# Gated cross-attention with a ternary FFN: the first two turns as one list, ternary weights by a sign, and spare TensorE products

## The reference

```
x = x + tanh(g_xattn) * attn(layernorm(x), ctx, ctx, mask)      # 16 heads of 32, 77 keys per batch
x = x + tanh(g_ffn)   * ffn(layernorm(x))

attn: q, k, v = query Wq^T, ctx Wk^T, ctx Wv^T;  softmax(masked q k^T / sqrt(32)) v;  times Wo^T
ffn:  down(silu(gate(z)) * up(z)), each a "bitlinear", 512 -> 2048 -> 512
  act_quant(x):    s = 127 / max(|x| over features); round(x s) clipped, / s
  weight_quant(w): s = 1 / mean(|w|); clip(round(w s), -1, 1) / s
```

## Time and profile before

| | us |
|---|---|
| median of 3 runs | 1346.26 (1342.62 to 1346.9) |
| profiled execution | 1347.23, of which the span of instructions is 1345.4 |
| TensorE (PE) busy | 1253.8 (93%) |
| VectorE (DVE) busy | 1122.8 (83%) |
| ScalarE (ACT) busy | 870.6 (65%) |
| GpSimd (POOL) busy | 737.6 (55%) |
| mean granted TensorE clock | 0.974 of full speed |

### The profile page before, as it was taken

One profiled execution on the slowest core, in us unless ns is written; L12 is line 12 of the kernel. 1 busy time (PEld: TensorE's weight loads), 2 busy tenths in 40 slices (PEclk: granted clock), 3 DMA queues, 4 the chain that ended last, 5 costly groups with the idle time before them and its releaser, 6 DMA issues.

```text
span 1345.4 us, 26267 instructions
## 1 busy us (share of the span) xinstructions
PE 1253.8 (93%) x7552; PEld 620.8 (46%) x8126; DVE 1122.8 (83%) x2631; ACT 870.6 (65%) x1350; POOL 737.6 (55%) x1186
## 2 busy tenths in 40 slices
PE   4767699999999999999999999999999999999996
PEld 2223344445454454545454454545445454544542
DVE  6777597897979898897979899797979889796883
ACT  4886756658584766757575665757475665857562
POOL 2104654647475564657466564757566465747662
PEclk9867899999999999999999999999999999999998
DMA  9785348565665658564674756565574847565432
GB/s 327 234 253 114 72 80 172 115 151 115 130 138 111 146 117 169 114 147 113 122 158 89 172 117 150 116 143 124 109 155 109 179 106 152 113 133 98 87 83 67
DMA packets 386793, 181.64 MB, mean 135 GB/s; under 512 B 324323, under 2 KB 357987, under 8 KB 385123
## 3 DMA queue, kind: packets, MB, share of 16 engines
q1 hardware_dynamic: 386736, 181.04, 60.0%
HBM read 61.32 MB, written 35.46 MB: 72 GB/s over the span
## 4 chain that ended last, share of the span: by engine, by line
PE 52%; DVE 18%; DMA 12%; issue 6%; ACT 5%; SPq 4%; POOL 2%; POOLq 0%; ACTq 0%; DVEq 0%
PE bank L1247 16%; PE bank L1259 11%; PE bank L1107 6%; PE bank L1108 6%; PE bank L1109 6%; DMA aT<-ah 6%; PE bank L1186 4%; DVE nmax L987 4%; DVE region L1048 3%; DMA xT<-xh 2%; DVE ah L1011 2%; DVE hmx L1054 2%; POOL work L621 1%; DVE xn L972 1%; ACT work L744 1%
## 5 line engine op out<-in xcount | busy, mean ns | idle before, releaser
L630 POOL TENSOR_TENSOR region<-region,up 128x512 f32<-128x512 f32 x256 | 328.4, 1288 | 290.9 <-DVE region L1048 197.6
L1247 PE MATMUL bank<-tern_gate,region 128*128 128x512 fp8e4 x1024 | 264.6, 381 | 12.3 <-DMA region<-zb 9.3
L1247 PE MATMUL bank<-tern_up,region 128*128 128x512 fp8e4 x1024 | 263.7, 380 | 0.8 <-ACT up L783 0.8
L1259 PE MATMUL bank<-tern_down,region 128*128 128x512 fp8e4 x1024 | 234.5, 382 | 13.7 <-DMA region<-hb 9.6
L1048 DVE SCALAR_TENSOR_TENSOR region<-region,bank 128x512 f32<-128x512 f32 x256 | 170.5, 679 | 79.5 <-ACT region L775 79.2
L775 ACT ACTIVATE region<-bank,fs 128x512 f32<-128x512 f32 x256 | 176.5, 693 | 65.7 <-PE bank L1247 65.6
L621 POOL TENSOR_TENSOR work<-work 124x512 f16<-124x512 f32 x160 | 184.4, 1172 | 26.9 <-ACT work L744 19.9
L1054 DVE TENSOR_REDUCE hmx<-region 128x1 f32<-128x512 f32 x256 | 170.1, 675 | 27.0 <-POOL region L630 26.9
L783 ACT ACTIVATE up<-bank 128x512 f32<-128x512 f32 x256 | 153.9, 602 | 38.0 <-PE bank L1247 37.9
L788 ACT ACTIVATE hb<-region 128x2048 bf16<-128x2048 f32 x64 | 122.8, 1919 | 43.8 <-DVE region L1070 43.8
L1259 PEld LDWEIGHTS bank<-tern_down,region 128*128 128x128 bf16 x1024 | 97.8, 98 | 109.9 <-issue 3.5
(11 more groups left out here) (145 smaller groups left out, 2357.1 us busy)
## 6 DMA issues: line engine op xcount, KB each, us to landing
q_stack<-q_rows SPq DMA_DIRECT2D x96, 256.0 KB, 4.4
xbig<-in_x SPq DMA_DIRECT2D x16, 1024.0 KB, 5.3
q_rows<-q SPq DMA_DIRECT2D x64, 256.0 KB, 3.2
out_y<-o SPq DMA_DIRECT2D x64, 256.0 KB, 3.2
q_stack<-mT SPq DMA_DIRECT2D x32, 256.0 KB, 4.2
region<-in_wgT SPq DMA_DIRECT2D x4, 1024.0 KB, 9.5
region<-in_wuT SPq DMA_DIRECT2D x4, 1024.0 KB, 7.4
region<-in_wdT SPq DMA_DIRECT2D x4, 1024.0 KB, 6.0
```

The source lines that it names most:

```text
L630: nc.gpsimd.tensor_tensor(ht, ht, up[:, n % 2, :], ALU.mult).then_inc(hmul_ready, 1)
L1247: ins = T.matmul(pb[2 * (n % 2) + w][:, :], xqT[:, k, tok], tern[w][:, k * FF + n * GT:k * FF + (n + 1) * GT], start=(k == 0), stop=(k == ...
L1259: ins = T.matmul(pb[2][:, :], hT[:, t % 2, k, :], tern[2][:, k * GT:(k + 1) * GT], start=(k == 0), stop=(k == FK - 1))
```

## The change

- Front and second turn are one list per engine. Part letters: B, C and K are A, N and Q of the second turn (groups 1, 2 and 2), F is the FFN of group 0. `second()` is gone. Steps of both turns may now be interleaved, and the order inside both is new.
- Of the weights, every quarter is scaled and rounded by one VectorE pass (times 1/mean plus MAGIC), and ScalarE makes the ternary value as the sign of (that minus MAGIC). The constant -MAGIC lies in column 38 of `con`, since the sign's bias is read from memory.
- `keep_busy` on TensorE: `W:hw33` does three products 128x512 into bank 3, `W:hw72` two into bank 7, whose results are never read. Eleven of the first stand behind the score maxima of group 0, nine of the second among the scores of group 0.
- In the front, TensorE does two q pieces of group 1 before the transpose of the maxima of group 0 (before: one) and all four before the scores. The transpose of group 1's maxima goes from behind the output projection to ahead of it. SyncE's list saves the keys (`ki`) before the first save of q and the first stack of keys, and group 0's last x transposes stand behind the first reload of a weight quarter.
- `m_split` waits on a semaphore of its own, and the numbering of VectorE's loop semaphore follows.

```diff
 TENSOR_FIRST = """
+    W:km00 W:vm00 R:q00 R:q10 R:q20 R:q30 R:s00 W:hw33 R:s01 W:hw33 R:s10 W:hw33 R:s11 W:hw33 R:s20 W:hw33 R:s21
+    W:hw33 R:s30 W:hw33 R:s31 W:hw33 W:hw33 W:hw33 W:hw33 Q:q00 Q:q10 R:mT00 Q:q20 Q:q30 A:sc00 W:hw72 Q:s00
+    A:sc01 W:hw72 Q:s01 A:sc02 W:hw72 A:sc03 W:hw72 A:sc04 W:hw72 Q:s10 Q:s11 A:sc10 W:hw72 Q:s20 A:sc11 W:hw72
+    Q:s21 A:sc12 W:hw72 Q:s30 A:pv00 A:sc13 W:hw72 A:pv01 A:sc14 Q:s31 A:pv02 A:pv03 A:pv10 A:pv11 A:pv12 A:pv13
+    Q:mT00 A:wo00 A:wo10 A:wo20 A:wo30 B:sc00 B:sc01 B:sc02 F:gu00 F:gu01 B:sc03 B:sc04 F:gu02 B:sc10 F:gu03
...
 SCALAR_FIRST = """
...
+    N:xh30 W:wt11 W:wt12 W:ws20 W:wt13 Q:q00 R:mT00 W:ws21 Q:q10 Q:q20 W:ws22 Q:q30 W:ws23 A:sc00 A:sc01 A:sc02
+    A:sc03 A:sc04 A:sc10 A:sc11 A:sc12 A:ah00 A:sc13 A:ah01 A:sc14 A:ah02 A:ah03 A:ah10 W:wt20 A:ah11 A:ah12
+    W:wt21 A:ah13 W:wt22 Q:mT00 W:wt23 A:zq00 A:zb00 B:sc00 B:sc01 B:sc02 A:zq10 F:up00 F:gu00 F:gu01 A:zb10
...
 VECTOR_FIRST = """
...
+    M:xl30 W:kp00 W:wr01 W:wr02 W:kc00 W:wr03 N:ln00 W:wl00 W:wx10 W:vm00 N:xn00 W:wp10 R:q00 N:xl00 N:xn10
+    N:xn20 R:q10 W:wm10 W:vp00 R:q20 R:q30 R:s00 R:s01 N:xl10 W:wr10 N:xl20 N:xn30 W:wr11 R:s10 R:s11 N:xl30
+    W:wr12 R:s20 R:s21 W:wr13 W:wl10 R:s30 R:s31 R:mh00 Q:q00 W:vc00 Q:q10 Q:q20 Q:q30 W:es00 W:wm20 Q:s00 Q:s01
...
 SYNC_FIRST = """
+    W:lx00 W:lc00 W:lk00 W:lz00 W:lw00 W:w00 W:w01 M:tx00 W:w02 W:w03 W:lv00 M:tx10 W:lx10 W:lw10 W:w10 M:tx20
+    M:tx30 W:w11 W:w12 W:w13 W:k100 W:ki00 R:qd00 W:k200 N:tx00 R:qd10 R:qd20 R:qd30 N:tx10 N:tx20 W:w20 N:tx30
...
-FRONT = "AMNRQW", {"A": 0, "M": 0, "R": 0, "N": 1, "Q": 1, "W": None}
+FRONT = "AMNRQWBCKF", {"A": 0, "M": 0, "R": 0, "N": 1, "Q": 1, "B": 1, "C": 2, "K": 2, "F": 0, "W": None}
...
             def weight_ternary(_, i, j):
 
-                act.wait_ge(wclip_ready, 4 * i + j + 1)
-                nc.scalar.activation(tern[i][:, j * FF:(j + 1) * FF], region[:, j * FF:(j + 1) * FF], ACT.Copy, bias=-MAGIC,
+                act.wait_ge(wround_ready, 4 * i + j + 1)
+                nc.scalar.activation(tern[i][:, j * FF:(j + 1) * FF], region[:, j * FF:(j + 1) * FF], ACT.Sign, bias=c(MINUS_MAGIC),
                                      saturate=False).then_inc(tern_ready, 1)
...
-            def weight_upper(_, i, j):
+            def weight_round(_, i, j):
 
                 dve.wait_ge(wmean_ready, i + 1)
-                V.tensor_scalar(region[:, j * FF:(j + 1) * FF], region[:, j * FF:(j + 1) * FF], c(R_G + i), 1.0,
-                                ALU.mult, ALU.min).then_inc(wupper_ready, 1)
...
+                V.tensor_scalar(region[:, j * FF:(j + 1) * FF], region[:, j * FF:(j + 1) * FF], c(R_G + i), MAGIC,
+                                ALU.mult, ALU.add).then_inc(wround_ready, 1)
...
+            def keep_busy(_, bank, n):
+                if bank == 3:
+                    pe.wait_ge(v_masked, B)
+                else:
+                    pe.wait_ge(mhl_ready, 1)
+                for k in range(n):
+                    T.matmul(pb[bank][:, :], wq_hi[:, 0, 0:P], wq_hi[:, 1, :], start=True, stop=True)
...
-            turn(TENSOR_ORDER, *second())
```

More of the change, by code:

```diff
@@ L107 @@
+    F:gu32 F:gu33 F:up32 B:zq30 F:up33 B:zb30 K:mT00
 """
 VECTOR_FIRST = """
[L109 to L112, removed]
@@ L117 @@
+    K:s10 K:s11 F:gu30 B:za30 F:gu31 K:s20 K:s21 F:gu32 F:gu33 F:hm30 K:s30 K:s31 F:hm31 K:mh00 F:hm32 F:hm33
+    F:down20 F:hs30
 """
@@ L286, in gated_cross_attention_and_ternary_ffn @@
         tern_in = [sem(f"tern_in{j}") for j in range(4)]
[L287 to L290, removed]
+        wsum_quarter, wmean_ready, wround_ready = (
+            sem(n) for n in ("wsum_quarter", "wmean_ready", "wround_ready"))
+        wsum_ready, wsum_all, tern_ready, gate_tanh, cast_ready, con_cleared = (
+            sem(n) for n in ("wsum_ready", "wsum_all", "tern_ready", "gate_tanh", "cast_ready", "con_cleared"))
         ln1_stats, ln1_rstd, xn_ready, xh_ready, xl_ready = (
@@ L531, in _ @@
             pieces["M"], pieces["R"] = pieces["N"], pieces["Q"]
+            pieces["B"], pieces["C"], pieces["K"] = pieces["A"], pieces["N"], pieces["Q"]
             pieces["E"] = pieces["G"] = pieces["H"] = pieces["I"] = pieces["F"]
@@ L539, in _ @@
             turn(SYNC_FIRST, *FRONT)
-            turn(SYNC_ORDER, *second())
             for g in range(2, NG - 1):
@@ L634, in _ @@
             pieces["M"], pieces["R"] = pieces["N"], pieces.get("Q")
+            pieces["B"], pieces["C"], pieces["K"] = pieces["A"], pieces["N"], pieces.get("Q")
             pieces["E"] = pieces["G"] = pieces["H"] = pieces["I"] = pieces["F"]
@@ L643, in _ @@
             turn(POOL_FIRST, *FRONT)
-            turn(POOL_ORDER, *second())
             with pool.Fori(2, NG - 1) as g:
@@ L792, in _ @@
                       "W": {"tn": gates_tanh, "oh": head_rows, "wh": projection_high, "kh": key_high, "vh": value_high,
-                            "vw": value_masks, "ws": weight_sum, "wu": weight_round, "wt": weight_ternary}}
+                            "vw": value_masks, "ws": weight_sum, "wt": weight_ternary}}
             pieces["M"], pieces["R"] = pieces["N"], pieces.get("Q")
+            pieces["B"], pieces["C"], pieces["K"] = pieces["A"], pieces["N"], pieces.get("Q")
             pieces["E"] = pieces["G"] = pieces["H"] = pieces["I"] = pieces["F"]
@@ L802, in _ @@
             turn(SCALAR_FIRST, *FRONT)
-            turn(SCALAR_ORDER, *second())
             with act.Fori(2, NG - 1) as g:
@@ L1085, in _ @@
                             "kp": key_scale, "kc": key_low, "vm": values_masked, "vp": value_scale, "vc": value_low,
-                            "es": score_scale, "ys": output_scale, "wm": weight_mean, "wu": weight_upper, "wc": weight_lower}}
+                            "es": score_scale, "ys": output_scale, "wm": weight_mean, "wr": weight_round}}
             pieces["M"], pieces["R"] = pieces["N"], pieces.get("Q")
+            pieces["B"], pieces["C"], pieces["K"] = pieces["A"], pieces["N"], pieces.get("Q")
             pieces["E"] = pieces["G"] = pieces["H"] = pieces["I"] = pieces["F"]
@@ L1095, in _ @@
             turn(VECTOR_FIRST, *FRONT)
-            turn(VECTOR_ORDER, *second())
             for g in range(2, NG - 1):
@@ L1264, in _ @@
                       "N": {}, "F": {"gu": gu, "down": down}}
-            pieces["W"] = {"km": keys_mm, "vm": values_mm}
+            pieces["W"] = {"km": keys_mm, "vm": values_mm, "hw": keep_busy}
             pieces["M"], pieces["R"] = pieces["N"], pieces.get("Q")
+            pieces["B"], pieces["C"], pieces["K"] = pieces["A"], pieces["N"], pieces.get("Q")
             pieces["E"] = pieces["G"] = pieces["H"] = pieces["I"] = pieces["F"]
```

75 lines of the change are left out of this document (36 added, 39 removed).

## The result

The changed kernel takes 1349.58 us (median of 7 runs, 1347.91 to 1350.93), the kernel before 1345.31 beside it: ratio 1.0035, 95% interval 1.0026 to 1.0044. The forecast was 1336, range 1326 to 1344. The profiled execution has a span of 1348.8 us against 1345.4. One profiled execution stands for each kernel, and it can lie up to 4.3 us from the kernel's median; where that matters it is said.

What follows compares the result with a forecast made beforehand. From 222 us TensorE's own stream bounds the kernel, so only the earlier part can be won. Gains of 8.2 + 1.5 + 1.0 = 10.7 us take the profiled 1347.2 to 1336.5, less 0.5 towards the median: 1336, range 1326 to 1344.

Steps and rivals of the forecast that it cites:

- Weights by a sign: Weight quantisation in the front: fewer VectorE and ScalarE passes, fourth x transpose landing 5 us earlier, bounds 0 and 8.
- Spare products: Behind the maxima and among the scores: 51 products keep the clock up for q products, 2.3 us gained, bounds -5.1 to +2.3.
- Hidden by the transpose's wait: Last four spare groups ahead of the next q products: 12 products, 2.6 us at the upper clock, counted as costing nothing.
- my signs of being wrong: First gate product later than 139, clock at 0.50 during the scores, or second turn above 82 us from its gate product.
- the largest gain: Softmax stage: four q pieces before the scores, first exponential near 92.3, ten chunks done at 104 instead of 111.6, 7.7 us.
- the row DMA has its time beside them: Maxima's rows, before the scores: their DMA fits beside two q pieces, which end at 89.3 after the maxima's transpose at 83.9.
- The tail of the front: Attention's transposes to the gate product: projection 5 to 7 us earlier, first gate product at 134.6 instead of 142.78, 8.2 us.
- One list: Second turn: three score chunks fill the 8.0 us wait before the gate product, 1.5 us; 1 us more from smaller waits.
- The change does not touch them: Thirteen middle turns and most of the last: TensorE's own stream, left as before at 76 to 77 us a turn.
- Table loads: Rival: the sign needs another table, four more ScalarE loads of 1.28 us, three on the path, 1340; chance 0.08.
- Spare products at the lower clock: Rival: clock stays 0.50 through maxima and scores, 14.9 us lost against 10.7 gained, 1351; chance 0.07.
- Gain spent on a wait: Rival: next x's transposes or the keys' save keep landing at 83, only softmax gains 4 to 5 us, 1342.5; chance 0.15.

Runs made afterwards that it cites:

- the last pair: Old first half, new second half, down-weight sums back in their old places, against the kernel before: two lists 1341.25 us (0.9964), one list 1342.73 us (0.9986).
- the one attempt to change the traffic: Changed kernel with SyncE's save of the keys issued behind the first batch's own key rows and the first q save: 1350.10 us, ratio 1.0041 to the kernel before.

## Why the prediction was wrong, step by step

*Weights by a sign.* Right in its counts and durations (1.28, 1.99, one table load). The fourth x transpose was issued at 76.08 and landed near 80, I had 78.5; TensorE started on it 2.1 us earlier, not 5, because the spare products ended only at 81.9. With the sign in the old lists the split of the maxima gained 7.1 us. So the sign was worth its 5 us at this point in the old lists (the q products start at 78.45 against 83.84), and the new order did not keep them. For the whole kernel the sign alone was worth nothing: 2.65 us at the end of the second turn, 2.6 given back in the steady turns.

*Spare products.* Their mechanism was right: clock 1.00 where it was 0.50. "Hidden by the transpose's wait" was not quite: the twelve ahead of the q products were the last thing TensorE waited for. They gain 2.7 us alone and 5 beside the sign in the old lists, more than the 2.3 that I gave them, and nothing in the new ones, where TensorE next waits for the maxima's rows. And two of my signs of being wrong came true: the clock was at 0.50 when the scores began, and the first gate product came later than 139.

*The step that failed* is the one that I called the largest gain: "three down-weight sums of 1.9 and two more q copies: the first exponential is at about 92.3", and the last at 104. They came at 98.75 and 115.8. The first is 6.5 us late, the last 11.8. Three things were missing. First, I placed the sums by their length on ScalarE and not by when their data land: the down weights were requested at 73.7 to 84.1 us, 3 to 7 us later than before, since a down quarter waits for the up quarter's ternary pass, and the new first half puts those among the maxima. The last one landed at 96.8, and both ScalarE's exponentials and GpSimd's sum stood behind it. Second, "the row DMA has its time beside them" took about the 4.2 us of the kernel before, where the DMA engines' share from 89.7 to 94.1 was 0.61; here it took 9.62, with a share of 1.09 from 87.9 to 97.6. It was the chain's largest piece here, and 8.69 us of it are in the chain of the kernel without the down weights' sum as well. No run changes this wait alone, so its own price stays open. Third, I knew GpSimd's start of 5.7 us and had the sum over the partitions in the list, but never asked what stands behind it: a gap of 6.67 us on the way back, for which the fifth chunk's exponential waits until 107.37; without the sum the last exponential comes at 112.27 instead of 115.83. Two things make that sum late. With the down weights early, it is the new place of ScalarE's sums and VectorE's mean behind the q pieces, and that place is worth 3.4 to 4.6 us. In the changed kernel itself it is the quarter's landing: VectorE was through with its q pieces at 94.1 and then waited 4.43 us. Taking the sum away there won about 2 us.

*The tail of the front.* It did move with the softmax, as I said, only the other way: projection 3.1 us late, gate product 3.5. I had also made the way from one to the other shorter, about 116 to 134.6, against 20.7 us before; it took 21.1, so that part of the 8.2 us had no ground either.

*One list.* The chunks do stand ahead of the first gate product, but it waits for the transposes all the same, 2.31 us behind them, and is no earlier. Three pairs of kernels have the one list 1.5 to 3.0 us slower. That its q rows and maxima go by DMA at the time of these transposes is what the rows show (a wait of 2.68 us for them in the last pair); that this is the cost isn't shown. The turn itself, 146.25 to 224.19, is 77.9 us: under the 82 that I set, and 0.6 shorter than before (78.5), where this part and the next term of my sum were to give 2.5.

*The steady turns.* "The change does not touch them": they lost 2.3 us in sum, a cost that I had put at nothing. Its cause is open. So where my sum has 8.2 + 1.5 + 1.0 us gained, the profiled execution has 3.5 lost up to the gate product, 0.6 gained in the second turn, 2.3 lost in the steady ones and 1.8 gained behind them: 3.4 us lost.

*The rivals.* Table loads: false. Spare products at the lower clock: false, but for 3.4 us. "Gain spent on a wait" named the right kind and the wrong place (transposes ahead of the q products; it was the maxima's rows and the down weights, needed after them), and stopped at 1342.5. The slower side had 0.07 on one mechanism that the trace already spoke against; the real one, lists that depend on each other through data with a landing time, had no case at all.

## What to carry to other kernels

When an order of work is rewritten, follow each moved step to its data and to what stands behind it on every engine: here a sum of 0.4 us on GpSimd came 6.6 us later, and the gap of 6.7 us behind it then held the softmax. Take edits apart before they are judged: sign and spare products together gave 0.9959, most or all of it from the spare products, and were buried by a new order that cost more than they won. And a better list for one engine is not better alone; parts of a good order for some engines, put under another order of the rest, cost 3 to 11 us.

## What the runs showed of the hardware

GpSimd is idle for 5.9 to 8.4 us between elementwise work and the maximum over partitions near 50 us in all 17 profiled kernels, and for 6.7 to 9.0 us between the sum near 95 us and the elementwise work behind it in the 16 that have this sum. In the one kernel without that sum, the last cross-partition work ends at 60.9, and the first low part starts at 98.44, 0.14 us behind its exponential: with much time between the two, nothing of the gap is left. On the way to the maximum the gap goes with the DMA engines' busy share over it: 5.9 to 6.3 us in ten kernels at shares of 0.43 to 0.56, 6.6 at 0.77, and 7.8 to 8.4 in six at 0.82 to 1.00. The rows of one of each kind, before and changed, over the gap (columns as above):

```profile
50.00:55.80 5.80, 4.01 (x18) 1.49 (x16) 3.15 (x4) 5.79 (x7) 0.01 (x1) 1.00 0.43 108
```

```profile
48.50:56.90 8.40, 4.30 (x20) 1.76 (x18) 2.61 (x2) 7.11 (x9) 0.02 (x1) 0.97 0.93 320
```

The Trainium skill, "GPSIMD Engine Reference", section "Instruction dispatch", says that the first call to newly loaded code pays a load of about 6 us; the gaps at a low DMA share agree, the others are up to 2.4 us above. That these gaps are such loads no trace here shows. That the DMA traffic is the cause isn't shown: all six have the new first half of SyncE's list and no other kernel has it; the way back, near 95 us, has gaps of 6.7 to 9.0 us with no such order (9.01 at 0.46, 6.80 at 0.88), and the one attempt to change the traffic left the share at 0.82 (0.93 in the changed kernel) and the gap at 8.01 us.
